# A routed two-layer block on one core: another order for the opening stage (merges, first two batches, x's first load)

## The reference

```python
# L0_cond: a feed-forward whose weights depend on the batch's expert id
hidden_i = x @ wi.T + 2 * (x @ common_wi_a.T) @ common_wi_b.T + lora(x, expert)      # 128 -> 512
hidden_o = relu(hidden_i) @ wo.T + 2 * (...common...) + lora(relu(hidden_i), expert)   # 512 -> 128
# L0_ffn: four rounds of a mixture of 4 experts, the best 2 for each token
for r in range(4):
    logits = flat @ Wg[r] + bg[r]; w = softmax(top2(logits))
    cur = cur + sum_e cw_e * (gelu(flat @ W1[e] + b1[e]) @ W2[e] + b2[e])
x = x + cur
# L1: a per-batch low-rank map, then a gated feed-forward with ternary weights
x = x + w3(gelu(h2(gelu(h1(silu(w1 z) * (w2 z))))))
```

## Time and profile before

| what | value |
|---|---|
| three runs | 482.44 us median, 481.11 to 483.73 |
| the profiled execution's own time | 480.89 us |
| its span | 479.1 us |
| PE busy | 474.2 us, 99% of the span |
| DVE busy | 386.7 us, 81% |
| ACT busy | 394.1 us, 82% |
| POOL busy | 121.8 us, 25% |
| TensorE's granted clock, mean | 1.00 of full |

### The profile page before, as it was taken

The page is one execution under the profiler, slowest core; times in us unless marked ns, Lnnn a source line. Parts: engine busy times, 40 slices in busy tenths (PEclk is TensorE's granted clock), DMA queues, the critical chain, the costliest instruction groups (busy, mean ns, idle before and its releaser), DMA issues.

```text
span 479.1 us, 7437 instructions
## 1 busy us (share of the span) xinstructions
PE 474.2 (99%) x2260; PEld 394.7 (82%) x2260; DVE 386.7 (81%) x638; ACT 394.1 (82%) x543; POOL 121.8 (25%) x102
## 2 busy tenths in 40 slices
PE   8999999999999999999999999999999999999997
PEld 7998888888888888888888888888888888888886
DVE  4898999999889898988889898889896758654343
ACT  4889888887889898888888798898888888697644
POOL 4995212121211212122212121171314144500000
PEclk9999999999999999999999999999999999999999
DMA  8604702021120202020202112120202000000002
GB/s 225 201 24 133 286 1 90 1 90 34 57 88 0 88 0 88 0 88 0 88 1 88 43 45 88 45 90 0 88 2 88 2 0 0 1 1 0 0 23 69
DMA packets 8299, 27.03 MB, mean 56 GB/s; under 512 B 2258, under 2 KB 3602, under 8 KB 6098
## 3 DMA queue, kind: packets, MB, share of 16 engines
q1 hardware_dynamic: 7090, 22.45, 13.5%
q0 software_dynamic: 288, 2.88, 1.7%
q10 hardware_dynamic: 896, 1.38, 1.1%
HBM read 25.26 MB, written 1.44 MB: 56 GB/s over the span
## 4 chain that ended last, share of the span: by engine, by line
PE 98%; DMA 1%; SPq 0%; DVE 0%; issue 0%
PE bank L538 34%; PE bank L541 34%; PE bank L544 26%; PE bank L565 1%; PE bank L638 1%; PE bank L639 1%; PE bank L599 1%; DMA stage<-lora_all 1%; PE bank L562 0%; PE bank L634 0%; DVE x L1312 0%; SPq L251 0%; SPq L356 0%; SPq L355 0%; SPq L354 0%
## 5 line engine op out<-in xcount | busy, mean ns | idle before, releaser
L859 ACT ACTIVATE act_out<-bank,vec 128x512 f32<-128x512 f32 x256 | 165.1, 683 | 40.0 <-PE bank L544 27.9
L1154 DVE TENSOR_TENSOR hid_lo<-act_out,hid_hi 128x1024 fp32r<-128x1024 f32 x128 | 157.5, 1249 | 32.8 <-ACT hid_hi L864 32.7
L864 ACT ACTIVATE hid_hi<-act_out 128x1024 fp32r<-128x1024 f32 x128 | 136.2, 1064 | 8.2 <-ACT act_out L859 0.4
L502 POOL TENSOR_TENSOR cur<-cur,prod 128x512 f32<-128x512 f32 x48 | 65.8, 1370 | 232.5 <-DVE prod L1165 232.1
L538 PE MATMUL bank<-hid_hi,moe_hi 128*128 128x512 f32 x256 | 99.8, 390 | 0.0
L544 PE MATMUL bank<-hid_hi,moe_lo 128*128 128x512 f32 x256 | 99.7, 390 | 0.0
L541 PE MATMUL bank<-hid_lo,moe_hi 128*128 128x512 f32 x256 | 99.7, 389 | 0.0
L538 PE MATMUL bank<-xhi,moe_hi 128*128 128x512 f32 x256 | 99.6, 389 | 0.0
L541 PE MATMUL bank<-xlo,moe_hi 128*128 128x512 f32 x256 | 99.6, 389 | 0.0
L544 PE MATMUL bank<-xhi,moe_lo 128*128 128x512 f32 x256 | 99.6, 389 | 0.0
L538 PEld LDWEIGHTS bank<-hid_hi,moe_hi 128*128 128x128 f32 x256 | 48.1, 188 | 11.0
(11 more groups left out here) (134 smaller groups left out, 568.8 us busy)
## 6 DMA issues: line engine op xcount, KB each, us to landing
cw_all<-cw_dram SPq DMA_DIRECT2D x16, 1024.0 KB, 4.7
stage<-ffn_w POOLq DMA_DIRECT2D x1, 2304.0 KB, 8.7
cw_all<-moe_w SPq DMA_DIRECT2D x4, 512.0 KB, 7.2
stage<-lora_all SPq DMA_DIRECT2D x5, 160.0 KB, 4.5
x<-x_t SPq DMA_DIRECT2D x3, 256.0 KB, 5.2
out_t<-x SPq DMA_DIRECT2D x3, 256.0 KB, 2.4
cur<-cond_base ACTq DMA_DIRECT2D x2, 256.0 KB, 3.6
stage<-ffn_w POOLq DMA_DIRECT2D x1, 512.0 KB, 4.0
```

The source lines that it names most:

```text
L502: pool.tensor_tensor(cur[:, c, :], cur[:, c, :], prod[:, s % 2, :], ALU.add).then_inc(add_done, 1)
L859: act.activation(act_out[:, f // 2, f % 2, :], bank[:, f, :], ACT.Gelu_apprx_tanh, bias=vec[:, V_B1 + e * FC + f:V_B1 + e * FC + f + 1]).t ...
L864: act.activation(hid_hi[:, s % 2, 2 * pr:2 * pr + 2, :], act_out[:, pr, :, :], ACT.Copy)\
L1154: dve.tensor_tensor(hid_lo[:, s % 2, 2 * pr:2 * pr + 2, :], act_out[:, pr, :, :], hid_hi[:, s % 2, 2 * pr:2 * pr + 2, :].bitcast(F32), ALU ...
```

## The change

The number of merges, products, sums and splits stays the same. What differs:

- the seven merge groups become six, most of them of three members, and the members of the last ones come later; the last two sums go to PSUM banks 0 and 1, which `cond_hidden` of even batches writes too, so `merge_group(5)` waits for `relu_low(4)` and `cond_hidden(6)` waits for the sums;
- TensorE does the hidden products of batches 0 and 1 right behind groups 0 and 1, cut into `first_high`, `first_x_low` and `first_low`, and group 2 after them;
- `cond_out(0)` and `cond_out(1)` stand ahead of `cond_hidden(2)`, and so on down the lists of PE, ACT, DVE and POOL;
- x's first chunk is issued on ACT's queue behind the lora tables of batch 1 instead of ahead of them, and the second half of the base weight ahead of batch 3's tables;
- the low half of x's second chunk (`x0_low(1)`) moves from POOL to DVE;
- eight products of zeros at the start instead of ten.

```diff
-                ((2, 0), (3, 0)),
-                ((2, 1), (3, 1)),
-                ((4, 0), (5, 0), (4, 1)),
-                ((6, 0), (7, 0), (5, 1)),
-                ((6, 1), (7, 1)))
+                ((2, 0), (3, 0), (2, 1)),
+                ((4, 0), (5, 0), (3, 1)),
+                ((6, 0), (4, 1), (5, 1)),
+                ((7, 0), (6, 1), (7, 1)))
-MERGE_BANKS = (6, 7, 2, 3, 5, 4, 6, 7, 4, 6, 7, 4, 6, 7, 4, 6)
+MERGE_BANKS = (6, 7, 4, 5, 6, 7, 4, 6, 7, 4, 4, 6, 7, 4, 0, 1)
-WARM, KEEP_WARM = 10, 4
+WARM, KEEP_WARM = 8, 4
...
                     pe.wait_ge(lang_in, 16)
+
+                    pe.wait_ge(relu_lo, 5)
...
             def cond_hidden(b):
...
+                if b == 6:
+                    pe.wait_ge(merge_free, max(summed_in(i, len(MERGED)) for i in range(2)))
...
             warm(KEEP_WARM)
+            first_high(0)
+            first_x_low(0)
+            first_high(1)
+            first_low(0)
+            first_x_low(1)
+            first_low(1)
             merge_group(2)
+            cond_out(0)
+            cond_out(1)
+            cond_hidden(2)
             merge_group(3)
-            first_hidden(0)
-            first_hidden(1)
+            cond_hidden(3)
+            cond_out(2)
+            cond_hidden(4)
             merge_group(4)
-            cond_out(0)
-            cond_hidden(2)
-            merge_group(5)
-            cond_out(1)
-            cond_hidden(3)
-            cond_hidden(4)
-            merge_group(6)
-            cond_out(2)
             cond_out(3)
             first_logits(0)
             cond_hidden(5)
-            cond_hidden(6)
+            merge_group(5)
             cond_out(4)
             cond_out(5)
+            cond_hidden(6)
             first_logits(1)
             cond_hidden(7)
             expert_in(0, 0, 0, (0,))
...
             base_load(act, 0)
-            x_load(act, 0)
             act.wait_ge(const_done, 1)
             act.activation(low_any[0:1, :], blank[0:1, 0:1], ACT.Gelu_apprx_tanh)
             act.wait_ge(ids_in, 16)
             first_load(act, 1)
+            x_load(act, 0)
+            base_load(act, 1)
             lora_load(act, 3)
-            base_load(act, 1)
```

More of the change, by code:

```diff
@@ L459, in _ @@
             merged_low(0, 1)
-            x0_low(1)
+            merged_low(1, 1)
             merged_low(2, 0)
-            merged_low(1, 1)
             merged_low(3, 0)
@@ L465, in _ @@
             merged_low(4, 0)
-            merged_low(4, 1)
             merged_low(3, 1)
@@ L469, in _ @@
             moe_low(0)
+            merged_low(4, 1)
+            merged_low(5, 1)
             merged_low(6, 0)
+            moe_low(4)
             merged_low(7, 0)
-            merged_low(5, 1)
             merged_low(6, 1)
-            moe_low(4)
             merged_low(7, 1)
@@ L583, in first_logits, with first_part, first_high, first_x_low @@
                 logits(c, gate_bank(c))
-            def first_hidden(b):
-                hi, lo, cols = mer_hi[:, b, 0, :], mer_lo[:, b, 0, :], batch_cols(b)
-                pe.wait_ge(mer_hi_done, HIGHS.index((b, 0)) + 1)
[L590 to L602, removed]
+            def first_part(b, weights, x, start=False, stop=False):
+                for f in range(FC):
+                    mm = pe.matmul(bank[:, 2 * b + f // 2, (f % 2) * SEQ:(f % 2 + 1) * SEQ], weights[:, f * P:(f + 1) * P],
+                                   x[:, 0, batch_cols(b)], start=start and f % 2 == 0, stop=stop, skip_group_check=True)
+                return mm
+            def first_high(b):
+                pe.wait_ge(mer_hi_done, HIGHS.index((b, 0)) + 1)
+                first_part(b, mer_hi[:, b, 0, :], xhi, start=True)
+            def first_x_low(b):
+                pe.wait_ge(x0_split[0], 1)
+                first_part(b, mer_hi[:, b, 0, :], xlo)
+            def first_low(b):
+                pe.wait_ge(mer_lo_done, LOWS.index((b, 0)) + 1)
+                first_part(b, mer_lo[:, b, 0, :], xhi, stop=True).then_inc(cond_h_done, 1)
             def cond_hidden(b):
@@ L955, in _ @@
             merged_high(0, 1)
+            relu_high(0)
             merged_high(1, 1)
+            relu_high(1)
+            merged_high(2, 0)
             x0_high(1)
-            relu_high(0)
-            merged_high(2, 0)
+            x0_high(2)
+            conditioned_high(0)
+            merged_high(3, 0)
+            conditioned_copy(0)
             merged_high(2, 1)
+            relu_high(2)
+            merged_high(4, 0)
+            relu_high(3)
             merged_high(3, 1)
[L962 to L969, removed]
+            merged_high(5, 0)
             x0_high(3)
             moe_high(0)
-            relu_high(3)
-            merged_high(5, 0)
+            relu_high(4)
+            merged_high(4, 1)
             moe_high(4)
+            conditioned_high(1)
+            merged_high(5, 1)
+            conditioned_copy(1)
             merged_high(6, 0)
[L976 to L981, removed]
             relu_high(5)
             lang_copy()
+            merged_high(7, 0)
+            merged_high(6, 1)
             moe_high(1)
[L985 to L988, removed]
             conditioned_high(2)
             conditioned_copy(2)
+            merged_high(7, 1)
+            relu_high(6)
+            moe_high(5)
+            moe_high(2)
             relu_high(7)
@@ L1250, in relu_low @@
                    .then_inc(relu_lo, 1)
-            split_gate()
+            merged_sum(0, 0)
             x0_low(0)
-            merged_sum(0, 0)
             merged_sum(1, 0)
@@ L1257, in _ @@
             merged_sum(1, 1)
+            split_gate()
+            relu_low(0)
             merged_sum(2, 0)
+            relu_low(1)
+            x0_low(1)
             merged_sum(3, 0)
             merged_sum(2, 1)
+            x0_low(2)
+            conditioned_low(0)
+            merged_sum(4, 0)
+            relu_low(2)
             merged_sum(3, 1)
-            relu_low(0)
-            merged_sum(4, 0)
-            merged_sum(4, 1)
             merged_sum(5, 0)
-            relu_low(1)
-            x0_low(2)
-            relu_low(2)
-            merged_sum(7, 0)
-            merged_sum(6, 0)
-            merged_sum(5, 1)
-            conditioned_low(0)
             relu_low(3)
             x0_low(3)
+            merged_sum(6, 0)
+            merged_sum(4, 1)
+            merged_sum(5, 1)
+            relu_low(4)
+            conditioned_low(1)
+            merged_sum(7, 0)
+            relu_low(5)
             merged_sum(6, 1)
             merged_sum(7, 1)
-            relu_low(4)
-            conditioned_low(1)
             gate_logits(0, 0)
-            relu_low(5)
             gate_order(0, 0)
+            conditioned_low(2)
             relu_low(6)
             gate_choice(0, 0)
-            conditioned_low(2)
             gate_gap(0, 0)
```

16 lines of the change are left out of this document (6 added, 10 removed).

## The result

| kernel | median of runs | ratio to before | 95% interval |
|---|---|---|---|
| before | 481.84 us (480.67 to 484.58) | 1 | |
| changed | 487.92 us (486.82 to 489.0) | 1.0126 | 1.0103 to 1.0149 |

The change costs 6.1 us, 1.3%. The forecast was slower by 3.3 us. The direction held.

What follows compares the result with a forecast made beforehand. TensorE was taken to bound the kernel, holding 98% of the chain. 0.1 (x) + 0.1 (merges) + 3.25 (handovers) - 0.15 gave +3.3 us: 484.2 profiled, 485.7 as median, range 483.6 to 488.0.

Steps and rivals of the forecast that it cites:

- The handovers: Between a batch's last hidden and first output product: too little other TensorE work covers relu_high and relu_low; +3.25 us.
- all seven terms: TensorE waits at batches 0, 1, 2, 3, cond_out(4), cond_out(5), batch 6: 0.45, 0.3, 0.4, 0.15, 0.25, 0.5, 1.2 us.
- The first rival: DVE's list: handovers covered better, only 1.15 of the 3.25 us stays; median 483.6; chance 0.28.
- x's load: Opening: x issued at 3.52, lands at 7.0 us (ends 6.3 and 9.0), first hidden product at 8.3; +0.1 us.
- x late: Opening: x lands 5.2 us after issue, at 8.7; 1.7 us more, 487.4; chance 0.10 together with a late clock.
- the port rule: x0_low(1) on DVE waits out a GpSimd instruction reading SBUF; could cost 1.95 us and batch 3 some 0.5 more.
- The clock: Opening: with zeros over at 4.6 the clock may rise late; 487.0 us; chance 0.10 together with x late.
- the forecast's own: The whole kernel: forecast as summed, slower by 0.5% to 1.1%, median 484.8 to 487.4 us; chance 0.59.
- x late or the clock late: Opening: x's landing or the clock's rise comes late, costing 1 us or more; chance 0.10.
- The sign: TensorE's opening: merge group 2 starting after 12.7 us would show the forecast wrong about x or the clock.
- The expert loop behind: After the first expert product: other engines shift with TensorE, which bounds it; no further wait, nothing made up.

Runs made afterwards that it cites:

- the two moved pieces back: Changed kernel with split_gate() at the front of DVE's list, x's load ahead of the ids and ten products of zeros: 484.73 us, 1.0071.
- x early: Changed kernel with x's first chunk issued ahead of the ids again, as before: 486.50 us, 1.0095.
- gate in front: Changed kernel with split_gate() back at the front of DVE's list: 487.76 us, 1.0116.
- ten zeros: Changed kernel with ten products of zeros instead of eight, nothing else: 488.29 us, 1.0128.
- `relu_low(6)` first: Changed kernel with split_gate() at DVE's front, x's load ahead of the ids, eight zeros, and relu_low(6) ahead of gate_order(0, 0) and conditioned_low(2): 487.02 us, 1.0116.

## Why the prediction was right, and where it was not

- **The handovers** (+3.25) were right in mechanism and size: 3.1 us in the trace with the two moved pieces back, all seven terms within 0.12 us, a single move (`cond_hidden(6)`) 2.0 us in the other kernel, and shortening `relu_low` takes the waits behind it from 2.6 to 0.6 us. The first rival, that DVE's slack covers them, is out.
- **x's load** was mis-sized. The term put the landing at 7.0 (issue + 3.5) with 6.3 and 9.0 as ends; it landed just ahead of 8.90, issue + 5.3, near the late end, so that the rival "x late" was the better forecast of that term. The first hidden product came 1.8 us later than forecast. The 2.6 us that the prediction takes from the Trainium skill, DMA: Bandwidth & Descriptors, the anatomy of one DMA, is a fit for the path of GpSimd; this load was issued by ACT, and no run here shows 2.6 for its size. I had also left out what the queue does to the load behind x: batch 3's tables. It stayed harmless in the changed kernel, and is what TensorE waits for when x and the base weight alone are moved in the kernel before.
- **`split_gate()`** was not in the sum at all. The part-by-part list names `x0_low(1)` as the piece that meets POOL and weighs the port rule against it, but the four small instructions that moved from a time with POOL idle to one with POOL at work got no term. In the changed kernel's trace they took 3.8 us instead of 0.87 and put 1.6 us ahead of `cond_out(0)`. This is the step that failed. Its price depends on what stands beside it: in the trace with x early it cost TensorE nothing, and the medians give it 0.2 to 0.5 us in the changed kernel, and 4.9 alone in the kernel before.
- **The clock.** The rival was right that it rises late with eight products of zeros (2.04 us for eight halves of zeros at 8 us), and that this lies mostly under the wait for x. It missed the dearer half: behind a wait on a fast TensorE the clock can fall again, at some 1.1 to 1.5 us a time (estimated from the rows). So the costs don't add. Taking one wait out leaves another ahead of a fall, and `split_gate()` in front won 0.2 to 0.5 us for 1.6.
- **The total.** 3.3 forecast, 6.1 measured. The trace's 8.1 is 3.3 and 1.8 (x), 0.2, 1.6 (`split_gate()`) and 1.2 (clock, 1.1 of it). How the 6.1 of the medians splits over the same causes can't be read from one execution. Undoing x, gate and zeros together gives 2.7 of it, each against its own before; what is left, 3.4, is what the forecast had summed. That the range held is luck in part: the median lies 0.1 us inside its end and above the forecast's own 484.8 to 487.4, in the case "x late or the clock late", to which I gave 0.10. The sign that I had named for it came: merge group 2 started at 13.68, after 12.7.
- **The expert loop behind** took the same time to 0.1 us, as forecast.

What stays open, besides the two executions without a fall of the clock: why all loads came later in the changed kernel. From 6 to 8 us its DMAs moved 172 GB/s against 259 before, with the same bytes in another order. No experiment separated the order of x, base weight and tables on the queue.

## What to carry to other kernels

When a hand-written order moves an instruction, ask which engine works beside it at its new place, for the smallest instructions too: here, a copy or cast of 0.2 us on VectorE next to GpSimd's splits took up to a whole split, 1.3 us, each time. Count for every producer and consumer pair how much other TensorE work stands between them and compare it with the length of the handover; that difference could be worked out from rows to within some tenths. And expect a wait of TensorE to cost more than its length where the clock falls behind it, as it did in seven of these traces, and such costs not to add up. A kept trace is one execution: compare what it says with the medians, and medians only with the kernel before of the same group.

## What the runs showed of the hardware that I had not expected

- Copies and casts of 16 to 128 columns on VectorE took 0.17 to 0.23 us with GpSimd idle and 0.95 to 1.29 beside it, ending within 0.1 us of GpSimd's instruction. A subtraction of 16 columns with both inputs in SBUF did the same: 0.17 and 1.15 us (`split_gate()` late in the kernel before).
- The granted clock fell to 0.50 behind waits of TensorE of 2.1 us (changed kernel), 2.3 (gate in front), 2.25 (ten zeros), 3.4 (`split_gate()` late in the kernel before) and 3.8 us (x late in it). It fell also behind waits of 1.0 and 1.4 us for the lora tables (x early; `relu_low(6)` first), both right behind the eight products of zeros, about 2 us after the wait had ended. It did not behind waits of 1.1 us further on, in the kernel before with `split_gate()` late and with thirteen zeros. So the length of the wait alone doesn't tell it.
- With one 256 KB load moved behind two of 80 KB on the same queue, it landed 5.0 to 5.9 us after its issue in four traces, against 3.6 to 4.4 in the traces with it in its old place. With x and the base weight moved alone, the last of that queue's loads came 3.7 us later.
